# Eight graph and expert sublayers on one core: bias products of full height, and retrieval work moved from VectorE to ScalarE and GpSimd

## The reference

```
v0, i0 = top_k(sim0, 16); v1, i1 = top_k(sim1, 16)
all_scores = v0[:, :, None] + i0[:, None, :]          # 16 x 16 sums
scores, picks = top_k(all_scores.reshape(256), 16)
h = gelu(q . down[picks]) * softmax(scores)
out += h @ up[picks]
```

## Time and profile before

| | |
|---|---|
| three runs | 447.56, 445.62, 447.5 us; median 447.5 |
| profiled execution | 447.06 us, of which the span of the instructions is 445.3 us |
| mean granted clock of TensorE | 0.969 |
| TensorE busy (matmul) | 411.0 us, 92% of the span |
| VectorE busy | 211.7 us, 48% |
| ScalarE busy | 123.7 us, 28% |
| GpSimd busy | 35.3 us, 8% |
| chain that ended last | TensorE 52% of the span, issue 5%, VectorE 2% |

### The profile page before, as it was taken

One profiled execution on the slowest core, in us unless ns is written; L12 is line 12 of the kernel. 1 busy time (PEld: TensorE's weight loads), 2 busy tenths in 40 slices (PEclk: granted clock), 3 DMA queues, 4 the chain that ended last, 5 costly groups with the idle time before them and its releaser, 6 DMA issues.

```text
span 445.3 us, 7553 instructions
## 1 busy us (share of the span) xinstructions
PE 411.0 (92%) x2791; PEld 309.9 (70%) x2791; DVE 211.7 (48%) x625; ACT 123.7 (28%) x353; POOL 35.3 (8%) x68
## 2 busy tenths in 40 slices
PE   7998999994669989999999999999999999999996
PEld 7598655884268868797795669656687995394482
DVE  5844454457994254563745546557432531111102
ACT  2312313313221112261443335342112222222130
POOL 4000010011232001001000010001000000000000
PEclk9999999999778999999999999999979899999999
DMA  8999579222001300799999999337200399999900
GB/s 287 395 422 338 207 279 390 110 96 94 0 2 43 146 0 3 307 396 419 419 324 305 353 421 316 100 118 305 101 1 0 116 428 422 419 419 421 411 10 24
DMA packets 19493, 104.31 MB, mean 234 GB/s; under 512 B 3537, under 2 KB 5457, under 8 KB 7808
## 3 DMA queue, kind: packets, MB, share of 16 engines
q1 hardware_dynamic: 19168, 103.81, 60.9%
q10 hardware_dynamic: 288, 0.02, 0.1%
HBM read 103.56 MB, written 0.26 MB: 233 GB/s over the span
## 4 chain that ended last, share of the span: by engine, by line
PE 52%; issue 5%; DVE 2%; ACT 1%; DMA 1%; POOL 0%; SPq 0%; POOLq 0%; DVEq 0%; ACTq 0%
PE ps L1145 9%; PE ps L1131 8%; PE ps L1810 6%; PE ps L1546 6%; PE ps L1535 3%; PE ps L1526 3%; PE ps L1629 3%; PE ps L1876 1%; DMA ew<-in_l_wq 1%; PE ps L1165 1%; PE ps L1650 1%; PE ps L1659 1%; PE ps L1156 1%; PE ps L1175 1%; PE ps L1637 1%
## 5 line engine op out<-in xcount | busy, mean ns | idle before, releaser
L1114 PE MATMUL ps<-ident 128*128 128x128 f32 x332 | 46.3, 294 | 2.7 <-POOL ident L660 2.7
L1114 PEld LDWEIGHTS ps<-ident 128*128 128x128 f32 x332 | 43.7, 208 | 5.2 <-POOL ident L660 2.7
L1145 PEld LDWEIGHTS ps<-y_t,ew 128*128 128x128 f32 x352 | 39.9, 192 | 1.7 <-issue 1.7
L1145 PE MATMUL ps<-y_t,ew 128*128 128x128 f32 x352 | 40.2, 275 | 0.0
L1131 PE MATMUL ps<-ew,y_t 128*128 128x512 f32 x72 | 32.7, 597 | 0.0
L1546 PE MATMUL ps<-y_t,ew 128*128 128x128 f32 x224 | 27.5, 277 | 0.0
L1546 PEld LDWEIGHTS ps<-y_t,ew 128*128 128x128 f32 x224 | 26.1, 192 | 0.8 <-issue 0.7
L797 ACT ACTIVATE prob_store<-ps,nmax_s 128x128 f32<-128x128 f32 x56 | 19.7, 384 | 14.5 <-DVE nmax_s L2002 14.5
L1131 PEld LDWEIGHTS ps<-ew,y_t 128*128 128x128 f32 x72 | 13.0, 190 | 13.5 <-issue 13.3
L2621 DVE SCALAR_TENSOR_TENSOR t<-prob_store 128x512 f32<-128x512 f32 x6 | 4.2, 693 | 36.4 <-ACT prob_store L1048 20.4
L733 POOL TENSOR_TENSOR ln_rstd<-ln_mv,minus_half 128x1 f32<-128x1 f32 x12 | 6.6, 550 | 126.9 <-DVE ln_mv L2375 126.9
(11 more groups left out here) (521 smaller groups left out, 759.1 us busy)
## 6 DMA issues: line engine op xcount, KB each, us to landing
ew<-in_l_w SPq DMA_DIRECT2D x20, 1024.0 KB, 21.8
dense<-in_l_w SPq DMA_DIRECT2D x12, 1024.0 KB, 21.2
ew<-in_l_wv SPq DMA_DIRECT2D x8, 1024.0 KB, 15.0
ew<-in_l_wk SPq DMA_DIRECT2D x7, 1024.0 KB, 15.5
ew<-in_l_wq SPq DMA_DIRECT2D x6, 1024.0 KB, 11.8
erows<-in_l_rows SPq DMA_DIRECT2D x4, 1280.0 KB, 12.3
ew<-in_l_wo SPq DMA_DIRECT2D x5, 1024.0 KB, 14.9
ew<-in_gqa_wq SPq DMA_DIRECT2D x3, 1024.0 KB, 10.4
```

The source lines that it names most:

```text
L1114: pe.matmul(ps[:, b, 3 * P:4 * P], ident[:], ident[:], start=True, stop=True)
L1145: last = pe.matmul(ps[:, b, m * n:(m + 1) * n], w[:, c, (first + m) * P:(first + m + 1) * P], in_t[:, c, 0:n], start=(c == 0), stop=(c == ...
```

## The change

Retrieval: the index cast goes to ScalarE. For heads 0 to 6 ScalarE also takes the exponent of `peer_rest` (0 where NEG stands, the same as `peer_exp` elsewhere), GpSimd subtracts the two, and ScalarE sums the difference; for head 7 the single operation on VectorE stays. The reciprocals of pairs of heads are formed at the end of a round. GpSimd makes both diagonals of heads 0 to 5, ScalarE that of head 6, VectorE that of head 7. On TensorE the residual products move from head 6 to head 4, and the identity products change from 10, 3 and 8 (ahead of heads 2, 4, 7) to 10, 8 and 3 (heads 2, 4, 6) and 2 behind head 7.

Attention: ScalarE copies `gat_l` and the counts. GpSimd prepares loops and the negative base of the cap, and VectorE makes the cap with one operation.

Graph convolution: the row of ones becomes `first_row`, 128x128 with ones in row 0 and zeros below; the bias rows are loaded late into row 0 of tiles of 128 rows (`qk_t` and `v`), whose other rows hold what was there. The identity products around the residual change from 3 and 3 to 8 and 2. At the norms of sublayers 6 and 8 one identity product more stands ahead of the transposes and one behind.

The diff, with like parts left out:

```diff
...
-SEARCH_STEPS = 6
-PICK_STEPS = 5
+SEARCH_STEPS = 5
+PICK_STEPS = 4
...
+        first_row = sb("first_row", [P, P])
+        gcn_rows = [qk_t[:, 0:CH, :].rearrange("p c n -> p (c n)"), qk_t[:, CH:2 * CH, :].rearrange("p c n -> p (c n)"),
+                    v[:, 0:D]]
...
+            sp.wait_ge(*at("l2_attended", 6))
+            for k, rows in enumerate(gcn_rows):
+                sp.dma_start(rows[0:1], A["gcn_b"][k:k + 1]).then_inc(sig("gcn_rows_landed"), 16)
...
+            pool.memset(first_row[:], 0.0).then_inc(sig("first_row_cleared"), 1)
...
+            pool.tensor_scalar(gat_cap[:], ident[:], -2.0 * GAT_NEG, GAT_NEG, ALU.mult, ALU.add).then_inc(sig("gat_loops_ready"), 1)
...
             layer_norm_rstd(0)
+            pool.wait_ge(*at("first_row_cleared", 1))
+            pool.memset(first_row[0:1], 1.0).then_inc(sig("first_row_ready"), 1)
...
-                pool.wait_ge(*at("peer_search_step", SEARCH_STEPS * (h + 1)))
+                pool.wait_ge(*at("peer_index_ready", h + 1))
...
+            def picked_weights(p):
+                pool.wait_ge(*at("peer_rest_ready", p + 1))
+                if p >= 4:
+                    pool.wait_ge(*at("peer_head_added", p - 3))
+                pool.tensor_tensor(peer_pick[:, p % 4, :], peer_exp[:, p % 4, :], peer_rest[:, p % 4, :], ALU.subtract) \
+                    .then_inc(sig("peer_picked"), 1)
+
+            def diagonals(k):
                 pool.wait_ge(*at("peer_inv_ready", k + 1))
-                if k:
-                    pool.wait_ge(*at("peer_head_added", 2 * k - 1))
-                pool.tensor_scalar(x1_t[:, 0, :], ident[:], pickinv[:, 2 * k:2 * k + 1], None, ALU.mult) \
-                    .then_inc(sig("peer_diag_ready0"), 1)
-
-            for h in range(H):
-                if h >= 4 and h % 2 == 0:
-                    diagonal((h - 4) // 2)
-                head_sums(h)
-            diagonal(2)
-            diagonal(3)
+                for p in (2 * k, 2 * k + 1):
+                    if k:
+                        pool.wait_ge(*at("peer_head_added", p - 1))
+                    pool.tensor_scalar(x1_t[:, p % 2, :], ident[:], pickinv[:, p:p + 1], None, ALU.mult) \
+                        .then_inc(sig(f"peer_diag_ready{p % 2}"), 1)
+
+            for n in range(H + 1):
+                if n < H:
+                    head_sums(n)
+                if n >= PICK_LAG:
+                    picked_weights(n - PICK_LAG)
+                if n >= PICK_LAG + 2 and n % 2 == 0:
+                    diagonals((n - PICK_LAG - 2) // 2)
             layer_norm_rstd(4)
...
+            act.wait_ge(*at("gat_s_projected", 1))
+            act.wait_ge(*at("gat_l_cleared", 1))
+            nc.scalar.copy(gat_l[0:H], ps[0:H, 2, 0:P]).then_inc(sig("gat_l_ready"), 1)
+            act.wait_ge(*at("gat_capped", 1))
+            nc.scalar.copy(cnt_sd[:], ps[:, 5, 0:P]).then_inc(sig("counts_ready"), 1)
...
+            def exp_of_sums(h):
                 act.wait_ge(*at("peer_pick_step", PICK_STEPS * h + 1))
...
+            def exp_of_rest(p):
+                act.wait_ge(*at("peer_pick_step", PICK_STEPS * (p + 1)))
+                nc.scalar.activation(peer_rest[:, p % 4, :], peer_rest[:, p % 4, :], ACT.Exp,
+                                     bias=negbest[:, p % 4:p % 4 + 1]).then_inc(sig("peer_rest_ready"), 1)
+
+            def sum_of_weights(p):
+                act.wait_ge(*at("peer_picked", p + 1))
+                nc.scalar.activation(peer_exp[:, p % 4, :], peer_pick[:, p % 4, :], ACT.Identity,
+                                     accum_out=picksum[:, p:p + 1]).then_inc(sig("peer_weights_summed"), 1)
+
+            def indices(h):
+                act.wait_ge(*at("peer_search_step", SEARCH_STEPS * (h + 1)))
+                nc.scalar.copy(topif[:, h % 4, :], topi[:, h % 4, :]).then_inc(sig("peer_index_ready"), 1)
+
+            for n in range(H + PICK_LAG):
+                p = n - PICK_LAG
+                if p >= 0:
+                    exp_of_sums(p)
+                if p >= 1:
+                    sum_of_weights(p - 1)
+                if 0 <= p < H - 1:
+                    exp_of_rest(p)
+                if n < H:
+                    indices(n)
...
+            act.wait_ge(*at("peer_inv_ready", H // 2))
+            act.wait_ge(*at("peer_head_added", H - 3))
+            nc.scalar.mul(x1_t[:, 0, :], ident[:], pickinv[:, H - 2:H - 1]).then_inc(sig("peer_diag_ready0"), 1)
...
-                if h in (2, 4):
-                    keep_clock(5, times=10 if h == 2 else 3)
-                if h == H - 2:
+                if h == 4:
                     pe.wait_ge(*at("gate_m_ready", 1))
                     residual_first((0, 1), 3)
+                if h in (2, 4, 6):
+                    keep_clock(5, times={2: 10, 4: 8, 6: 3}[h])
                 if h == H - 1:
-                    keep_clock(5, times=8)
-                pe.wait_ge(*at("peer_pick_step", PICK_STEPS * (h + 1)))
+                    pe.wait_ge(*at("peer_pick_step", PICK_STEPS * H + 1))
...
+            keep_clock(5, times=2)
...
-            keep_clock(7, times=7)
+            keep_clock(7, times=8)
             layer_norm_transpose(5)
+            keep_clock(0, times=1)
...
-                    pe.matmul(ps[:, b, 0:D // 2], ones[32 * (k // 2):32 * (k // 2) + 1, :],
+                    pe.matmul(ps[:, b, 0:D // 2], first_row[:],
                               gcn_rows[k][:, half * D // 2:(half + 1) * D // 2], start=True, stop=False)
-            keep_clock(1, times=3)
+            keep_clock(1, times=8)
             pe.wait_ge(*at("x_updated", 6))
             for half, b in enumerate(gcn_out[2]):
                 pe.matmul(ps[:, b, 0:D // 2], ident[:], x[:, half * D // 2:(half + 1) * D // 2], start=False, stop=False)
-            keep_clock(1, times=3)
+            keep_clock(1, times=2)
...
-            dve.tensor_copy(gat_l[0:H], ps[0:H, 2, 0:P]).then_inc(sig("gat_lr_ready"), 1)
...
-            dve.tensor_copy(cnt_sd[:], ps[:, 5, 0:P]).then_inc(sig("counts_ready"), 1)
-            dve.tensor_tensor(gat_cap[:], ps[:, 5, 0:P], ident[:], ALU.add)
-            settle()
-            dve.tensor_scalar(gat_cap[:], gat_cap[:], 1.0, -2.0 * GAT_NEG, ALU.min, ALU.mult)
-            settle()
-            dve.tensor_scalar(gat_cap[:], gat_cap[:], GAT_NEG, None, ALU.add)
+            dve.wait_ge(*at("gat_loops_ready", 1))
+            dve.scalar_tensor_tensor(gat_cap[:], ps[:, 5, 0:P], -2.0 * GAT_NEG, gat_cap[:], ALU.mult, ALU.add) \
+                .then_inc(sig("gat_capped"), 1)
...
-                if search:
-                    searched(h, 5)
-                    dve.tensor_copy(topif[:, b, :], topi[:, b, :]).then_inc(sig("peer_search_step"), 1)
-                if pick:
+                if p >= 2 and p % 2 == 0:
+                    dve.wait_ge(*at("peer_weights_summed", p))
+                    dve.reciprocal(pickinv[:, p - 2:p], picksum[:, p - 2:p]).then_inc(sig("peer_inv_ready"), 1)
+                if p == H - 1:
                     picked(p, 4)
-                    dve.wait_ge(*at("peer_exp_ready", p + 1))
-                    if p >= 4:
-                        dve.wait_ge(*at("peer_head_added", p - 3))
+                    dve.wait_ge(*at("peer_exp_ready", H))
...
             for n in range(H + PICK_LAG):
...
-            weight_sums(H - 1, H)
-            dve.wait_ge(*at("peer_inv_ready", H // 2 + 1))
+            dve.wait_ge(*at("peer_pick_step", PICK_STEPS * H + 1))
+            dve.wait_ge(*at("peer_weights_summed", H - 1))
+            dve.reciprocal(pickinv[:, H - 2:H], picksum[:, H - 2:H]).then_inc(sig("peer_inv_ready"), 1)
...
```

More of the change, by code:

```diff
@@ L886, in _ @@
             act.preload_act_table(ACT.Exp)
-            def diagonal(k):
-                act.wait_ge(*at("peer_inv_ready", k + 1))
-                if k:
-                    act.wait_ge(*at("peer_head_added", 2 * k))
-                nc.scalar.mul(x1_t[:, 1, :], ident[:], pickinv[:, 2 * k + 1:2 * k + 2]).then_inc(sig("peer_diag_ready1"), 1)
-            for h in range(H):
+            def exp_of_sums(h):
                 act.wait_ge(*at("peer_pick_step", PICK_STEPS * h + 1))
@@ L2023, in _ @@
             settle()
-            dve.memset(gat_l[32:40], 1.0)
+            dve.memset(gat_l[32:40], 1.0).then_inc(sig("gat_l_cleared"), 1)
             dve.wait_ge(*at("x_landed", 16))
```

37 lines of the change are left out of this document (15 added, 22 removed).

## The result

| | before | after |
|---|---|---|
| runs | 445.62 to 447.56 us, median 446.94 (4) | 439.57 to 440.35 us, median 440.15 (4) |
| profiled execution, span | 447.06, 445.3 us | 439.57, 437.8 us |
| mean granted clock | 0.969 | 0.983 |
| VectorE, ScalarE, GpSimd busy | 211.7, 123.7, 35.3 us | 207.6, 131.3, 40.9 us |

The ratio is 0.985, with a 95% interval of 0.9823 to 0.9877: 5.5 to 7.9 us faster. Forecast: 441.0, in a range of 438.0 to 444.5. The profiled pair (the two executions whose profiles are read here) lies 7.5 us apart where I had summed 6.0.

The account below looks back on a forecast made before the run. Retrieval was taken as bound by VectorE until 135.8 us, then TensorE, whose half clock counts in full in convolution and router; 447.06 - 0.2 (start) - 3.5 (retrieval) - 1.5 (convolution) - 0.8 (router) gave 441.0 us, range 438.0 to 444.5.

Parts of the forecast that it names:

- Retrieval, VectorE: Head loop: cast and weights leave VectorE, full rounds 3.8 to 3.3 us, VectorE through 2.2 us earlier.
- T: Start of the first pick-only round in the retrieval, forecast at 127.8 us instead of 130.83.
- Retrieval, TensorE: Residual and identity products move ahead of head 4's product into empty time; net -4.0 or -1.4, taken as -3.5 us.
- full-clock case: Retrieval on TensorE at full clock: first half of head 7 done at 135.2 instead of 139.61, 4.4 us earlier.
- half clock: Retrieval on TensorE at half clock: first half of head 7 done at 137.6, 2.0 us earlier.
- VectorE's 2.2 us: Retrieval: how much earlier VectorE was forecast to be through, net of the stall in the first pick-only round.
- Convolution: Graph convolution: full-height bias passes keep TensorE's clock; mixing starts 1.0 us earlier and is 0.5 shorter, together -1.5 us.
- Rival B: Gate goes by busy time alone, or the stand before x drops it: convolution and router 0, 443.3 us; 16%.
- Router: Final router: added identity products at the norm keep TensorE busier against the half clock; bounds 0 and -1.6, taken -0.8 us.
- Start: Attention stage at the start: later first norm against VectorE's saved copies and cap operations; net -0.2 us, bounds +0.5 and -0.7.

Follow-up runs that it names:

- retrieval_te_old: The changed kernel with TensorE's order of before in the retrieval, VectorE's part untouched; median 442.82 us, ratio to before 0.9921.
- bias_one_row: The changed kernel with the convolution's six bias products made from one row again, 8 and 2 identity products kept; median 441.25 us, ratio to before 0.9895.
- gcn_identities_3_3: The changed kernel with 3 and 3 identity products around the convolution's residual, full-height biases kept; median 440.16 us, ratio to before 0.9877.
- norms_without: The changed kernel without the identity products added at the norms of sublayers 6 and 8; median 440.02 us, ratio to before 0.9872.

## Why the prediction was right

The time was inside the range and 0.9 from the forecast; the mechanisms were right in two of four terms, retrieval and convolution. These two are 5.9 us of the 7.5 measured. The other two, 1.0 of the 6.0 forecast, rested on mechanisms that the runs refute; that they did not spoil the number is luck.

- **Retrieval, VectorE.** Right: rounds of 3.3 us, T at 127.47 for 127.8, no wait in full rounds, a stall of 0.76 for 1.1. The subtraction took 0.73 for the 0.7 taken. The slack in a full round is 0.6, not 0.2: the sum's last part ends at 123.31 + 0.19 = 123.5, the reciprocal starts at 124.12.
- **Retrieval, TensorE.** The full-clock case came: 135.2 worked out, 134.96 measured. The term, -3.5, was mis-sized twice. It was drawn toward the half clock, and it charged 0.4 for the two identity products behind head 7; the output products start 0.39 behind z_t now and 0.35 before, so they cost next to nothing. Measured -4.5 in the profiled pair. retrieval_te_old shows how the two parts hang together: VectorE's 2.2 us came through only with TensorE's order.
- **Convolution.** -1.5 forecast, -1.4 measured, by the steps named: residual 1.12 for 2.07, mixing behind the scaled matrix (wait 0.68), 1.13 for 1.91. One step was half wrong, without effect: twelve full-height passes take 2.6 us against before's 1.92. Height is not why, since one-row passes from row 0 alone take 2.78 (bias_one_row). Before's operands lay in rows 0 and 32, and the trace has its first eight passes start in pairs 0.01 us apart; that this made them quicker is likely and not tested. Either way they end before x comes.
- **Rival B.** The rule of the Trainium skill, page "TensorE: Matmul & The Clock Gate" (What's actually happening), that the gate goes by how busy the engine has been, isn't enough here: the clock fell in stretches busy 2.00 of 2.00 us with one and with 32 rows, and held with 128 rows at 1.06 busy of 2.00 (318 to 320 in gcn_identities_3_3).
- **Router.** The step that failed: "One more identity product ahead and one in the gap keep it busier". norms_without keeps the clock without them. The 1.5 of the profiled pair are those of an execution that had the fall; 13 of before's 50 later runs lie about 1.5 us below the rest, so these need not have had it. Full-height biases alone were enough for the clock to hold at the router in the one profile taken; why is open.
- **Start.** -0.2 is refuted: +0.1 to +0.3, inside the bounds. The step that failed is that the first minimum's time carries on to the stage's end. The first minimum did start earlier (15.41 for 16.15), but the update of x did not. The cap's base took 0.30 us, not 0.61.

## What to carry to other kernels

Where TensorE's clock falls though the engine is busy, look at how many rows its products fill before adding more of them: padding a one-row product to 128 rows of zeros was worth 1 to 3 us here by the interval, five more identity products nothing. Work taken off an engine counts only as far as the next engine's queue order lets it through; ask which queue sets the end, and reorder that one. And compare profiles from an instant shared by both kernels, and only executions of the same form: a single pair gave the wrong sign for the start and the wrong cause for the router.

## What the runs showed of the hardware

- Twelve passes on 1 or 32 of 128 rows were followed by a fall of TensorE's clock from 2.4 to 1.2 GHz, while the profile shows it busy throughout, in all four profiled executions; the same passes on 128 rows, 127 of them multiplied by zeros, in none of ten.
- fp32 passes of 256 columns start 0.216 us apart on 128 rows (12 in 314.68 to 317.27) and on one row (four in 316.48 to 317.34, bias_one_row). Before's twelve, with operands in rows 0 and 32, took 0.16 each (319.31 to 321.23).
- GpSimd scaled and shifted a 128x128 matrix in 0.30 us with immediate numbers; scaled by a column of scalars it took 0.608.
- The start's first transposes take 0.6 or 1.1 us in executions of either kernel while the granted clock reads 1.00; what sets which is open.
